# Routed adapters: the differences of the up factors and of b_up are taken on VectorE, SyncE issues every load, and the raw down weight stands whole on chip

## The reference, cut to what matters

```
h = gelu(x @ W_down[type] + b_down[type])          # 1024 -> 512
y = x + h @ W_up[type] + b_up[type]                # 512 -> 1024
y = (y - mean(y)) / sqrt(var(y) + 1e-5)
x = y * gamma[type] + beta[type]
```

## Time and profile before

| | us |
|---|---|
| median of 3 runs (lowest, highest) | 2823.11 (2822.96, 2826.91) |
| the profiled execution's own time | 2828.77 |
| its span from first to last instruction | 2826.8 |
| PE, DVE, ACT, POOL busy | 2711.9, 2159.2, 1689.6, 1422.4 |

### The profile page before, as it was taken

One profiled execution on the slowest core, in us unless ns is written; L12 is line 12 of the kernel. 1 busy time (PEld: TensorE's weight loads), 2 busy tenths in 40 slices (PEclk: granted clock), 3 DMA queues, 4 the chain that ended last, 5 costly groups with the idle time before them and its releaser, 6 DMA issues.

```text
span 2826.8 us, 56889 instructions
## 1 busy us (share of the span) xinstructions
PE 2711.9 (96%) x11714; PEld 2216.2 (78%) x11714; DVE 2159.2 (76%) x3321; ACT 1689.6 (60%) x2907; POOL 1422.4 (50%) x956
## 2 busy tenths in 40 slices
PE   7899999998899999999989999999889999999997
PEld 5688888887788888888768888888667888888885
DVE  4677777766777777777788888888787888888886
ACT  3566666565565656666556565666555655656565
POOL 2455555555555555555454444444354444444446
PEclk9999999999999999999999999999999999999999
DMA  6565666666565656666666666656666666666663
GB/s 186 176 202 191 218 205 210 209 222 212 189 209 195 224 197 211 205 207 206 213 200 212 203 207 196 222 192 215 203 197 205 213 199 202 207 192 219 208 203 146
DMA packets 366261, 574.33 MB, mean 203 GB/s; under 512 B 41216, under 2 KB 241024, under 8 KB 365696
## 3 DMA queue, kind: packets, MB, share of 16 engines
q1 hardware_dynamic: 363968, 563.31, 61.5%
q0 software_dynamic: 1728, 6.29, 0.8%
HBM read 364.97 MB, written 204.47 MB: 201 GB/s over the span
## 4 chain that ended last, share of the span: by engine, by line
PE 82%; issue 7%; DVE 5%; POOL 1%; DVEq 1%; ACT 1%; DMA 1%; SPq 1%; POOLq 1%; ACTq 0%
PE pD L492 44%; PE bX L504 22%; PE bZ L504 16%; DVE xt L852 1%; DVE wul L769 1%; DVEq L222 1%; DVE hl L834 1%; DVE xt L875 1%; DVE wdl L752 0%; DVE xt L844 0%; DMA rwd<-in_Wd 0%; DVE xl L812 0%; POOL rwu L408 0%; POOL rwu L415 0%; ACT wdh L550 0%
## 5 line engine op out<-in xcount | busy, mean ns | idle before, releaser
L440 POOL TENSOR_TENSOR xt<-xt,cgb 128x1024 f32<-128x1024 f32 x260 | 699.8, 2692 | 342.9 <-ACT xt L662 341.6
L492 PE MATMUL pD<-wdh,xh 128*128 128x512 f32 x2080 | 818.9, 394 | 48.8 <-DVEq L796 40.4
L492 PE MATMUL pD<-wdl,xh 128*128 128x512 f32 x2080 | 815.1, 392 | 0.0
L492 PE MATMUL pD<-wdh,xl 128*128 128x512 f32 x2080 | 814.1, 391 | 0.0
L662 ACT ACTIVATE xt<-xt,rstd 128x1024 f32<-128x1024 f32 x260 | 298.9, 1150 | 383.1 <-POOL rstd L433 303.0
L492 PEld LDWEIGHTS pD<-wdh,xh 128*128 128x128 f32 x2080 | 394.6, 190 | 140.9 <-DVEq L796 49.5
L492 PEld LDWEIGHTS pD<-wdh,xl 128*128 128x128 f32 x2080 | 394.0, 189 | 83.0
L492 PEld LDWEIGHTS pD<-wdl,xh 128*128 128x128 f32 x2080 | 394.7, 190 | 81.4
L875 DVE SCALAR_TENSOR_TENSOR xt<-xt,nmean,cgb 128x1024 f32<-128x1024 f32 x260 | 441.4, 1698 | 0.0
L448 POOL TENSOR_TENSOR cs<-hT 128x256 f32<-128x256 f32 x130 | 97.1, 747 | 681.7 <-DVE hT L819 679.2
L504 PE MATMUL bX<-wuh,hh 128*128 128x512 f32 x1040 | 410.8, 395 | 27.7 <-DVE xt L844 21.5
(11 more groups left out here) (91 smaller groups left out, 3798.8 us busy)
## 6 DMA issues: line engine op xcount, KB each, us to landing
xq<-in_xB SPq DMA_DIRECT2D x130, 512.0 KB, 3.7
htok<-hg SPq DMA_DIRECT2D x260, 256.0 KB, 2.8
hq<-htok SPq DMA_DIRECT2D x1040, 64.0 KB, 2.3
xt<-in_x SPq DMA_DIRECT2D x130, 512.0 KB, 4.2
mid<-xt SPq DMA_DIRECT2D x130, 512.0 KB, 3.9
xq<-mid SPq DMA_DIRECT2D x520, 128.0 KB, 3.2
xt<-mid SPq DMA_DIRECT2D x130, 512.0 KB, 4.1
out<-xt SPq DMA_DIRECT2D x130, 512.0 KB, 2.7
```

The lines of the kernel that those rows point to most:

```text
L440: eng.tensor_tensor(xt[:, k, :], xt[:, k, :], cgb[:, 1, :], ALU.add).then_inc(s_o, 1)
L492: last = eng.matmul(pD[e][:, :], a[:, e, 128 * k:128 * k + 128], w[:, k, :], start=False, stop=(k == 7 and n == 2), skip_group_check=True)
```

## The change

- `rwd` grows from half of the down weight to all of it (128x8x512). One function, `down_weights`, issues its eight DMAs and the one of b_down at the place where `first_weights` stood; the late `down_rest` is gone from SP's step. `low_wd` has no wait and increment between its parts.
- Two blocks `t2` and `t4` (tile `twu`) are added, so that two differences don't overwrite b12.
- The four factor differences and the difference of b_up move from POOL to DVE: two in a new conditional `factors(w)` behind `low_h(w, 0)` in `begin`, that of b_up in `take_wu_0`, and two in `take_wu_1`.
- b_up, gamma and beta are loaded by SP (`up_biases`, `gains`), each in a conditional of its own in SP's step.
- sqrt(H) multiplies rstd (128x2) on POOL for each pair, instead of gamma once in each phase. POOL's step keeps one conditional of three and loses its two drains; the semaphore that `scale` waits for (`s_cg`) is incremented on POOL behind `sums` of the same step, one step later than before.
- `steps` sets the number of turns from the engine's own distance to the end: DVE and ACT get ten turns in the second layer instead of nine, SP keeps nine.
- The scratch space for software DMAs shrinks to 512.

```diff
-        rwd = sb("rwd", [128, 2, 2, K])
+        rwd = sb("rwd", [128, 8, K])
+        twu = sb("twu", [128, 2, 2, K])
...
+            for first in (6, NP + 5):
+                for c in range(low, first):
+                    body(Pair(c))
+                turns = (first // NP * NP + NP - ahead - first) // M
+                with eng.Fori(0, turns) as j:
...
-                when_new(eng, i + 1, down_rest)
+                when_new(eng, u, gains)
                 if (i + 1).first():
                     up_weights(i + 1)
+                    up_biases(i + 1)
+                if not v.first():
+                    when_new(eng, v, up_biases)
...
+                    count(eng, s_rs, p, 2, 1)
+                    eng.tensor_tensor(rstd[:, n:n + 2], rstd[:, n:n + 2], rooth[:, 0:1].broadcast_to([128, 2]), ALU.mult)\
                        .then_inc(s_rs, 1)
...
-                u, w = i + -3, i + -2
+                w, z = i + -2, i + -4
                 sums(w)
-                norm(u + -1)
-                if w.exists():
-                    when_new(eng, w, take_bu)
-                    eng.drain().then_inc(s_cb, 1)
-                shift(u + -1, 0)
-                when_new(eng, w, factors)
-                shift(u + -1, 1)
-                if u.exists():
-                    when_new(eng, u, take_gb)
-                    eng.drain().then_inc(s_cg, 1)
+                if z.exists():
+                    when_new(eng, z, take_gb)
+                    eng.sem_inc(s_cg, 1)
+                norm(z)
+                shift(z, 0)
+                shift(z, 1)
...
+            def factors(p):
+                c = pt.next()
+                eng.wait_ge(s_ru, c * 128 + 128)
+                eng.tensor_tensor(b12, b12, b11, ALU.subtract).then_inc(s_sub, 1)
+                eng.wait_ge(s_sub, c * 4 + 1)
+                eng.tensor_tensor(t2, b22, b12, ALU.subtract).then_inc(s_sub, 1)
+                eng.wait_ge(s_sub, c * 4 + 2)
+                eng.sem_inc(s_seen, 1)
...
                 low_wu(c * 7, 1, b12)
+                eng.wait_ge(s_bu, c * 16 + 16)
+                eng.tensor_tensor(cbu[:, K:H], cbu[:, K:H], cbu[:, 0:K], ALU.subtract).then_inc(s_bz, 1)
...
+                low_wu(c * 7, 2, t2)
                 low_wu(c * 7, 3, b22)
+                eng.tensor_tensor(t4, b21, t2, ALU.subtract).then_inc(s_sub, 1)
+                eng.wait_ge(s_wul, c * 7 + 1)
+                eng.tensor_tensor(b11, t2, b11, ALU.subtract).then_inc(s_sub, 1)
...
                 low_h(w, 0)
+                when_new(eng, w, factors)
```

More of the change, by code:

```diff
@@ L122, in routed_adapters @@
             "s_it", "s_io", "s_id", "s_p", "s_oh", "s_pc", "s_ctl"))
-        s_rd = [sem(f"s_rd{k}") for k in range(3)]
+        s_rd = [sem(f"s_rd{k}") for k in range(2)]
         s_ru = sem("s_ru")
@@ L174, in count, with steps @@
                 eng.wait_ge(s, p.times(per, plus))
[L176 to L190, removed]
+        def steps(eng, body, low, high, ahead):
+            for first in (6, NP + 5):
[3 more added lines that the diff above has]
+                with eng.Fori(0, turns) as j:
+                    for m in range(M):
+                        body(Pair(first + m, j))
+                low = first + M * turns
+            for c in range(low, high):
                 body(Pair(c))
@@ L245, in routed_adapters @@
         b11, b12, b21, b22 = (rwu[:, g, :, n, :] for g in range(2) for n in range(2))
+        t2, t4 = (twu[:, n, :, :] for n in range(2))
         block = ctx.enter_context(nc.Block())
@@ L262, in item, with down_weights, up_biases, gains @@
                 return eng.value_load(c_ord[0:1, bass.ds(s, 1)], min_val=0, max_val=NB - 1)
[L264 to L281, removed]
+            def down_weights(p):
+                row, c = adapter(p), pd.next()
+                eng.wait_ge(f_rd, c + 1)
+                for h in range(2):
+                    for a in range(4):
+                        r = 256 * a + 128 * h
+                        eng.dma_start(rwd[32 * a:32 * a + 32, 4 * h:4 * h + 4, :],
+                                      Wd[row, r:r + 128, :].rearrange("a (k i) n -> (a i) k n", i=32))\
+                           .then_inc(s_rd[h], 16)
                 count(eng, s_sd, p + -1, 2, 2)
                 eng.dma_start(cbd[:, :], bd[row, :].broadcast_to([128, K])).then_inc(s_bd, 16)
[L285 to L288, removed]
+            def up_biases(p):
+                row = adapter(p)
+                count(eng, s_sx, p + -1, 1, 1)
+                eng.dma_start(cbu[:, :], bu[row, :].broadcast_to([128, H])).then_inc(s_bu, 16)
+            def gains(p):
+                row = adapter(p)
+                count(eng, s_o, p + -1, 2, 2)
+                eng.dma_start(cgb[:, 0, :], ga[row, :].broadcast_to([128, H])).then_inc(s_gb, 16)
+                eng.dma_start(cgb[:, 1, :], be[row, :].broadcast_to([128, H])).then_inc(s_gb, 16)
             def up_weights(p):
@@ L396, in _ @@
             pg = Phases(eng, "pl_gb")
[L397 to L419, removed]
             def take_gb(p):
-                row = adapter(p)
-                count(eng, s_o, p + -1, 2, 2)
-                eng.dma_start(cgb[:, 0, :], ga[row, :].broadcast_to([128, H])).then_inc(s_gb, 16)
-                eng.dma_start(cgb[:, 1, :], be[row, :].broadcast_to([128, H])).then_inc(s_gb, 16)
                 eng.wait_ge(s_gb, pg.next() * 32 + 32)
-                eng.tensor_tensor(cgb[:, 0, :], cgb[:, 0, :], rooth[:, 0:1].broadcast_to([128, H]), ALU.mult)
+                eng.sem_inc(s_seen, 1)
             def norm(p):
@@ L692, in end @@
                 square(u, 1, 1)
-            steps(eng, halves(begin, end), -1, NPH + 5)
+            steps(eng, halves(begin, end), -1, NPH + 5, 0)
         @block.vector
```

46 lines of the change are left out of this document (26 added, 20 removed).

## The result

| | before | changed |
|---|---|---|
| median of 6 runs each (us) | 2823.37 | 2834.35 |
| lowest to highest | 2821.42 to 2826.91 | 2833.26 to 2835.43 |
| profiled execution, its span | 2828.77, 2826.8 | 2833.26, 2831.4 |

The ratio is 1.0037 (95% interval 1.0024 to 1.0049): 11.0 us slower, where 20.9 was forecast. The profiled execution of before stood 5.4 us above its median, so the two traces differ by less than the medians. The kernel before was therefore profiled again (2820.26 us, span 2818.5); against that trace the changed one is 12.9 us longer.

A forecast was written before the change was run, and what follows sets the result against it. PE's pace was taken as the floor, so only interruptions could move. Conditional 13.6, tenth turn 2.75, multiplication 2.7, down weights -2.6 and up weights 4.4 sum to +20.9 us: median 2844.0, range 2829 to 2855.

The forecast's parts named there:

- the ninth seam: Layer 2, DVE's second loop with ten turns: one more jump back, 1.9 us plus 0.85 for the conditional, 2.75 us slower.
- start and tail: Start gains on the down weight, loses on b_down and `factors`; tail has two more conditionals: zero together, -3 to 3 us.
- the forecast's other terms: Down weights -2.6 us, up weights +4.4 us, and start and tail zero together.
- The conditional at the seam: Untaken conditional ahead of DVE's jump back, covered in ordinary pairs but not at 16 seams: 0.85 us each, 13.6 us slower.
- The multiplication of rstd: POOL, each pair: 0.3 us, delaying `shift`, v5 and product 6 behind nine layer 2 seams, 2.7 us slower.
- Rival 1: Behind layer 2 seams, DVE's `scale` starts before POOL's `shift` and takes 1.28 us; saves 9.5 us, median 2834.5; 20%.
- Down weights: Weight phases: earlier whole-weight load gains 1.6 us at pair 95 and 0.5 each at 30 and 65, together -2.6 us.
- Up weights: Weight phases: v4 3.7 us later, v4 to v1 1.75 shorter, net 1.95 in layer 2; sum +4.4, range -5 to 12.
- the collision with `shift`: In `take_wu_0`, POOL's `shift` falls into DVE's work and holds it 2.25 us of v4's 3.7 us delay.
- Rival 2: The conditional is covered at the seam and `take_wu_0` has no collision with `shift`: about no change, 2824 us; 12%.
- rival 3: Factor differences off POOL clear the phases, v4 before product 5 asks: 8 us saved per phase, 24 in all, 2816; 8%.
- Rival 4: b_down or raw up weight late at phases, or a second fetch stall each turn in a larger loop body: 2856; 10%.

## Why the prediction was right or wrong, point by point

- **The sign and the main cause were right, the size was not.** 20.9 us were forecast and 11.0 measured. Against before (the mean of its two profiles), PE's pairs say where: the 16 old seams cost 9.1 us where the conditional and the multiplication were to cost 16.0 there, the ninth seam 2.85 where 3.05 was forecast; start and tail gave 4.0 where zero stood; the three changes of weights cost 0.1 where 1.8 was forecast. The two errors, at the seams and at the start, fell on the same side; the range was wide enough for both.
- **Taking the three costs out** is the other way to count them: 13.6 + 2.75 + 2.7 = 19.05 were forecast, and without them the kernel takes 17.7 us less. By PE's pairs the seams give 14.3 and the phases 4.9, and the start takes 2.3 back. That kernel is 7.3 below the before of its group (2816.70 against 2824.05), where the forecast's other terms came to -2.6 + 4.4 + 0 = +1.8.
- **The conditional at the seam** (0.85 us, 16 times) was priced rightly: 0.97 against 0.15 us from `low_h` to the end of the jump is 0.82, and nothing covers it, as the empty conditional in before shows (19.3 us for 16). The failed step is the silence behind it, which the forecast took to stay as long as it was. It is shorter in the changed kernel, 3.05 us in layer 1 and 3.15 in layer 2 against 3.6 and 3.5, which gives back about half of the conditional. So the seam pairs of layer 1, forecast 0.85 longer, are 0.3 to 0.4 longer than before (20.99 against 20.68 and 20.59), and 0.58 longer than in the kernel without the conditional. Why it is shorter stays open.
- **The ninth seam**, 2.75 forecast: 2.85 in the pair, 2.4 in the medians.
- **The multiplication of rstd.** `shift` comes 0.28 later and `scale` lasts 0.28 more; 0.3 was forecast. The order of the two stayed, as the sum had it. (The prediction calls the other order its second rival at this place; in its list it is the first.) The medians give 5.6 for it where 2.7 was forecast; the seam pairs explain 2.2 to 3.3, and where the rest lies stays open.
- **Rival 1 has the right time for the wrong reason.** It gave 2834.5, and the median is 2834.35, but by its mechanism `scale` would be 1.28 behind the seams of layer 2, and it is 3.38 at every one of them. That order exists, but in layer 1 and before the change as after it. The agreement in the time is chance.
- **Down weights.** At phase 95 the wait at down(i,0,2) fell from 6.41 to 2.70 us, and a new one stands at down(i,0,0), 4.32 for ACT's write of b_down against 1.14 before. The forecast saw the bias late behind twice the DMAs and took 0.6 for it; it is 3.2. With product 2's wait between the two (1.11 before, none now) the waits fell by 1.6, but the pair is hardly shorter: 32.07 us against 32.27, and 31.31 in before's second profile. At the two other changes the pair with the down weights is 29.24 and 29.12 us against 30.73 and 30.27, where 0.5 each was forecast. So the total of -2.6 is about met (-2.2 against the mean of before's two profiles), with another share at each change. With the bias issued earlier the median falls by 3.0.
- **Up weights.** v4 was to come 3.7 later and came 3.3 later (12.94 against 9.61 behind `low_h`), the collision with `shift` included, and product 5 waited 3.33 more (6.14). From v4 to the next v1 it was to be 1.75 shorter and is 2.56 shorter (14.78 against 17.34), so product 2 nearly doesn't wait (0.59 against 3.26). The mechanism held, step by step; its net was +1.95 for a phase in layer 2 and is 0.8 here. Behind it down(i,0,2) waits 5.43 us, which the forecast left out; it was 4.64 before and 5.08 in the second profile. That three phases together cost the 4.4 can't be told from none, since they differ by 2 to 3 us each between two executions.
- **The start** stood with the tail at zero, from -3 to 3, without a sum for either, and is the second step that failed: 5.9 us are gained at the start in the changed kernel's trace, 3.9 in that of the kernel with nine turns. Two parts: the second half of the first down weight isn't waited for (2.85 to 0.30), which the kernels with the loads alone show too (product 0 is 2.8 and 2.4 us earlier there), and POOL's four differences no longer hold up the first up product (6.11 to 3.02, and 3.02 with nine turns too). The forecast worked this out for the phases and not for the start, where DVE has no other work beside them. The tail lost 1.8 us of it (2.3 with nine turns).
- **What would show it.** Seam pairs of 23.4 in layer 2 were 23.15, but those of layer 1 grew by 0.35 and not by 0.85; the wait at down(i,0,2) of phase 95 was to be 4.2 and is 2.70 in the changed kernel and 4.13 in the one with nine turns; product 5 over 5 us and product 2 nearly none are there. Rival 2 fell with the empty conditional, rival 3 with v4. Rival 4's second stall isn't in the changed kernel, but it exists: the kernel with the loads alone had it.

## What to carry to other kernels

Price an instruction at a hardware loop's jump back as if nothing covered it: the sequencer is silent there for more than 3 us, and whatever stands ahead of the jump adds to it. Look for fewer jumps before a better order of work: turns of twelve pairs gave more than the whole change lost. After any edit, look at the silences behind the jump first: one that came double here was a matter of where the code lies, it cost more than most edits, and eight idle instructions ahead of the loops ended it. A chain of work hides what ran beside something else: read the length of a conditional from the rows of its source line. When work moves off a shared engine, work out the start with the same care as the steady part.

## What the runs showed of the hardware that was not expected

- A jump back can have two silences (3.64 and 3.33 us) with one instruction between them. It was so at all eight seams of one loop and at none of the other loop, and eight instructions ahead of the loops ended it: 36 us by the medians, 21 by the two profiles.
- A conditional that isn't taken costs DVE's sequencer 0.81 us, of which the flag load from SBUF is 0.31 (never under 0.297 in the 774 of the changed kernel). Put into the kernel before at the jump back, it added in full.
- The silence behind a jump back is 3.05 to 3.79 us as the mean of a loop, by the kernel and the loop, and differs between the turns of one loop by up to 1.2; what sets it isn't known.
- A POOL multiplication of 128x2 takes 0.20 us (0.214 as a mean of 130), the power of the same size 1.68.
- `scale` is held for as long as POOL's `shift` lasts: 3.10 to 3.13 us without the multiplication and 3.37 to 3.40 with it at every seam of layer 2, in all fourteen traces. Where it starts ahead of `shift`, at every seam of layer 1, it takes 1.28.
